# A graph network on one core: sums over edge slots moved from a VectorE reduce to TensorE, with constant waits in the gather loops

## The chip, the cores and the metric

One NeuronCore of one Trainium2 chip runs the whole program in one launch. The metric is the device time of that launch in microseconds, the lower the better. The engines have short names in what follows: PE is TensorE, DVE is VectorE, ACT is ScalarE, POOL is GpSimd, SP is SyncE. Each has its own instruction queue; they wait for each other by semaphores only.

## The reference, cut to what matters

A graph of 6250 nodes and 206,250 edges (each of 100,000 random pairs in both directions and a loop on every node), sorted by destination, passes through four layers. Layer one is a graph attention layer applied twice (4 heads of 32 columns):

```
h = x @ W;  e = leaky_relu(alpha_s[src] + alpha_d[dst], 0.2)
e_exp = exp(e - segment_max(e, dst)[dst])
alpha = e_exp / (segment_sum(e_exp, dst)[dst] + 1e-16)
out = segment_sum(h[src] * alpha, dst)          # then elu, the second time a residual and a layernorm
```

The second layer sums source rows weighted by edge weights, `segment_sum(x[src] * edge_weight, dst)`, with dense products on both sides of it; the third is an attention layer with 8 heads of 16 columns over the same edges; the fourth is an MLP on each edge, with batch norms over all edges, summed by destination.

## The kernel before, in words

Nodes are ordered by the number of their edges and cut into 49 tiles of 128, one node on a partition. A tile's edges stand in slots, and slots in groups of four (`J`), so that a group is four table rows for each of 128 nodes. A tile has as many groups as its fullest node needs: 15 for the first, then fewer. All tiles together have 428.

`Gather` serves all four gather stages. POOL issues four indirect DMAs a group into a ring of eight groups (L820), waiting for the slots' indices and for `used`, by which the consumer gives a place back. SP waits until a group has landed, raises `landed` (L838) and loads indices for two groups at a time from the DRAM table `slot_src` (L831). That table is laid out by group, then partition, so that an index load reads 16 bytes at a time. The waits compare a semaphore that only grows with a count that is computed in registers (`hold`, L106 and L107, or `wait_ge(sem, g + 1)`).

`attention_pass` is the consumer in layer one and in the attention layer. Its softmax runs: for each group DVE computes scores (L1159 and L1161 in layer one, L1439 and L1441 in the attention layer), weighs the rows of the group before with exponents (`weigh_rows`, L1022, four slots at once), rescales the old sum (`weigh_sum`, L1028) into a fifth slot, takes the maximum (L1037), adds the five slots up (`add_up`, a reduce, L1034), and subtracts the maximum (L1040). ACT takes the exponent (L1094) and copies the new maximum (L1096). At a tile's end DVE divides (L1075 to L1077) and adds the bias (L1165); the next tile begins at L1152. Each tile reads its number of groups and its first group from tables by register loads.

In layer one `DenseRows` works beside it on the second layer's dense weight matrix: for each tile and each chunk of 64 edges a node (here one chunk a tile) it builds one-hot tiles on DVE (L905 to L918), scales them by the edge weights on ACT (L965) and multiplies them on PE (L938) into eight PSUM banks, 32 pairs of slots; each application of layer one does one half of the 64. ACT copies the banks out (L974) and stores them (L978), and fetches the next column of edges (L945). ACT's order in a tile is: the tile's exponents, the store of the tile before, the fetch, the scalings. Nothing else stands between, so the exponents of the next tile come behind the scalings. DVE's order is the tile's groups, then its one-hot tiles. PE has only the dense products.

`edge_stats` is the gather stage of the edge layer: PE transposes gathered rows (L1664), DVE adds (L1645) and takes statistics (L1650), ACT stores. `sum_by_source` multiplies the stored weight matrix with the rows.

## Time and profile before

| | us |
|---|---|
| median of 3 runs (13887.12 to 13893.61) | 13889.23 |
| profiled execution | 13903.95 |
| its span, first to last instruction | 13902.3 |
| DVE busy | 8362.2 (60%) |
| POOL busy | 7297.4 (52%) |
| PE busy | 3796.4 (27%) |
| ACT busy | 2966.8 (21%) |

The rows below come from the one profiled execution. Times are microseconds from the span's start unless marked ns. An engine is busy while an instruction works; register, branch, semaphore and DMA-issuing instructions don't count as busy. A group of instructions is written as line, engine, operation, `out<-in`, count; then busy us and mean ns of one; then the idle time of the engine just before them, and what ended it. `<-issue` is idle time for which no releaser is seen. A timeline row is start, duration, engine, line, operation, and merges what follows without a gap (xcount). A name with a q (ACTq, DVEq) is an engine's sequencer.

### The profile page before, as it was taken

What the parts mean: (1) busy time and instruction counts of PE and PEld (TensorE: products, weight loads), DVE (VectorE), ACT (ScalarE), POOL (GpSimd) and SP (SyncE); (2) the same over time, 40 slices, a digit from 0 to 9 for tenths busy, and PEclk for the clock granted to TensorE, in tenths of its full rate; (3) what the DMA queues carried; (4) which work ended last, traced back from release to release, by engine and by line L of the source; (5) the groups of instructions that cost most, each with busy time, mean ns of one, the idle gap of its engine ahead of it and who ended that gap; (6) DMA issues with size and microseconds to landing.
All of it is one profiled execution on the core that took longest, in us unless ns stands there. A gap on an engine that the chain in (4) does not pass through costs nothing. (4 is left out here: it accounts for less than half of the span.)

```text
span 13902.3 us, 141045 instructions
## 1 busy us (share of the span) xinstructions
PE 3796.4 (27%) x15301; PEld 2288.4 (16%) x15400; DVE 8362.2 (60%) x19005; ACT 2966.8 (21%) x8231; POOL 7297.4 (52%) x7734
## 2 busy tenths in 40 slices
PE   2011122223322222233861000000422222229673
PEld 1001112222211222222431000000221111113221
DVE  7663677777657777774024777777533333346785
ACT  0410233333312333331000000000000000007693
POOL 0103777766467776660004777777137777760132
PEclk9999566666655566666975555555655555559996
DMA  0011334434324444442732444444123333337673
GB/s 2 10 21 30 80 92 96 97 97 98 92 59 93 97 95 100 93 102 94 258 135 55 106 106 105 106 106 107 29 66 106 105 105 106 106 99 244 183 218 89
DMA packets 1268796, 1386.52 MB, mean 100 GB/s; under 512 B 501892, under 2 KB 938986, under 8 KB 1255816
## 3 DMA queue, kind: packets, MB, share of 16 engines
q0 software_dynamic: 276128, 650.85, 19.1%
q1 hardware_dynamic: 500200, 404.68, 10.3%
q10 hardware_dynamic: 492416, 330.48, 8.2%
q14 instruction: 43, 0.35, 0.0%
q8 instruction: 9, 0.15, 0.0%
HBM read 1009.64 MB, written 375.70 MB: 100 GB/s over the span
## 5 line engine op out<-in xcount | busy, mean ns | idle before, releaser
L820 POOL DMA_INDIRECT ring<-gat_table,index x3424 | 3277.9, 957 | 1421.4 <-issue 1004.1
L820 POOL DMA_INDIRECT ring<-kv_table,index x1712 | 1739.9, 1016 | 531.5 <-issue 509.9
L820 POOL DMA_INDIRECT ring<-b_table,index x1712 | 1617.0, 945 | 599.0 <-issue 518.5
L1034 DVE TENSOR_REDUCE acc<-prod 128x132 f32<-128x660 f32 (+1 forms) x1284 | 1709.8, 1332 | 5.1
L1022 DVE TENSOR_TENSOR prod<-ring,p 128x528 f32<-128x528 f32 (+1 forms) x1284 | 921.1, 717 | 623.6 <-ACT e L1096 598.4
L938 PE MATMUL pairs<-hot_lo,hot_hi 128*128 128x128 f32 x6272 | 949.4, 325 | 1238.1 <-ACT hot_lo L965 1237.7
L1094 ACT ACTIVATE p<-x 128x20 f32<-128x20 f32 (+1 forms) x1284 | 286.7, 223 | 4350.1 <-DVE x L1040 4350.1
L965 ACT ACTIVATE hot_lo<-hot_lo,wt 128x128 f32<-128x128 f32 x3136 | 927.9, 387 | 999.5 <-remote 981.7
L938 PEld LDWEIGHTS pairs<-hot_lo,hot_hi 128*128 128x128 f32 x6272 | 924.7, 239 | 1290.5 <-issue 1289.1
L932 PE MATMUL pairs<-nil 128*128 128x512 bf16 x686 | 342.3, 598 | 2315.3 <-ACT dstage L974 2267.2
L1922 PE MATMUL e<-r,fc 128*128 128x512 f32 x1712 | 894.1, 626 | 289.5 <-ACT r L1934 133.5
L1645 DVE TENSOR_TENSOR tb<-bt,att 128x512 f32 x428 | 295.9, 691 | 1111.4 <-PE bt L1664 1054.0
L1664 PE MATMUL bt<-ident,ring 128*128 128x128 f32 x1712 | 465.2, 427 | 1683.5 <-SPq L838 1657.3
L1837 POOL DMA_DIRECT2D running<-run x432 | 232.6, 539 | 997.5 <-DVEq L1887 580.3
L712 PE MATMUL tp<-ident,stage 128*128 128x128 f32 x294 | 73.5, 427 | 2442.0 <-DVEq L699 2390.4
L1934 ACT ACTIVATE r<-tb,coef 128x512 f32<-128x512 f32 x854 | 674.6, 809 | 135.1 <-DMA tb<-kept 103.0
L1664 PEld LDWEIGHTS bt<-ident,ring 128*128 128x128 f32 x1712 | 306.1, 217 | 1842.9 <-issue 1842.9
L577 POOL DMA_INDIRECT layer_out<-by_node,node x49 | 46.3, 944 | 1018.5 <-PEq L86 1003.9
L1254 PE MATMUL fsum<-mat,xs 128*128 128x448 f32 x1372 | 545.1, 549 | 116.4 <-DMA ring<-gat_table,index 89.8
L918 DVE TENSOR_TENSOR hot_lo<-lo,ramp 128x512 f32<-128x512 f32 x784 | 563.1, 718 | 0.0
L1439 DVE TENSOR_TENSOR qk<-ring,qt 128x544 f32<-128x544 f32 x428 | 309.3, 723 | 393.1 <-SPq L838 369.4
L916 DVE TENSOR_TENSOR hot_hi<-hi,ramp 128x512 f32<-128x512 f32 x784 | 533.8, 681 | 3.4
(343 smaller groups left out, 8128.7 us busy)
## 6 DMA issues: line engine op xcount, KB each, us to landing
tb<-kept SPq DMA_DIRECT2D x856, 256.0 KB, 3.0
dense_weights<-dstage ACTq DMA_DIRECT2D x196, 1024.0 KB
mat<-dense_weights SPq DMA_DIRECT2D x98, 1568.0 KB, 6.2
kept<-tb ACTq DMA_DIRECT2D x432, 256.0 KB, 2.2
ring<-gat_table,index POOLq DMA_INDIRECT x3424
running<-run POOLq DMA_DIRECT2D x432, 64.0 KB, 2.9
ring<-kv_table,index POOLq DMA_INDIRECT x1712
ring<-b_table,index POOLq DMA_INDIRECT x1712
```

The costliest lines, as they stand in the source:

```text
L820: pool.indirect_dma_start(self.ring[:, at, :], None, self.table, bass.IndirectOffsetOnAxis(self.index[:, at:at + 1], 0)).then_inc(self.g_s ...
L916: dve.tensor_tensor(self.hot_hi[:, four, :], self.hi[:, four].unsqueeze(2).broadcast_to(shape), ramp, ALU.is_equal)
L918: dve.tensor_tensor(self.hot_lo[:, four, :], self.lo[:, four].unsqueeze(2).broadcast_to(shape), ramp, ALU.is_equal).then_inc(self.marked[b ...
L932: pe.matmul(self.ps[:, b, :], self.nil[:, 0:P], self.nil[:, :], start=True, stop=False, skip_group_check=True)
L938: mm = pe.matmul(self.ps[:, b, i * P:(i + 1) * P], self.hot_hi[:, 4 * b + i, :], self.hot_lo[:, 4 * b + i, :], start=False, stop=False, sk ...
L965: last = act.activation(self.hot_lo[:, i, :], self.hot_lo[:, i, :], ACT.Copy, scale=self.wt[:, i:i + 1])
L1022: dve.tensor_tensor(by_head(prod[:, 0:J, :]), by_head(ga.group(g)[:, :, 0:VB]), p5[:, 0:J, :].unsqueeze(3).broadcast_to([P, J, heads, dim ...
L1034: return dve.tensor_reduce(acc[:, :], prod[:, :, :].rearrange("p s c -> p c s"), AX.X, ALU.add)
L1254: mm = pe.matmul(acc[:, m, 0:MM], xs[:, u, :], mat[:, u, m * MM:(m + 1) * MM], start=start, stop=start, skip_group_check=True)
L1664: mm = pe.transpose(bt[:, r, j * P:(j + 1) * P], ga.ring[:, (first + r) * J + j, :], k.ident[:, :])
L1922: pe.matmul(e1[:, r, :], fc[:, :], r4[:, r, :], start=True, stop=True).then_inc(product, 1)
L1934: act.activation(r4[:, slot, :], tb[:, slot, :], ACT.Relu, bias=coef[:, 1:2], scale=coef[:, 0:1]).then_inc(relued, 1)
```

## The change

Five edits, made together.

1. In `attention_pass` the reduce over five slots goes. `prod` has two buffers, the sum stands in two PSUM banks (`acc`), and PE adds with five products by the identity matrix, four as soon as the rows are weighed and the fifth when the old sum is rescaled. DVE gives the ring's place back after the rescaling, reads the old sum from PSUM, and at a tile's end waits for PE.
2. PSUM has eight banks, so `DenseRows` keeps four: `PAIRS` goes from 32 to 16, and each application of layer one works through two units of 16 pairs a tile instead of one of 32. The column is fetched once for each unit, and the first unit is stored between the two.
3. In the gather loops a wait is for a constant, and takes what it waited for off the semaphore (`claim`). The first group and first chunk of a tile are no longer read from tables but counted in a register (`Running`).
4. `slot_src` is laid out by partition, so that an index load is 64 contiguous bytes a partition and covers four groups, and the writes of the slot stage are 256 contiguous bytes.
5. The same waits are changed in `edge_stats`, `edge_regather`, `build_slots` and `sum_by_source`.

The diff, cut to its core:

```diff
 NBLK = NP // BLK
-PAIRS = 32
+PAIRS = 16
 QUADS = PAIRS // 4
...
+
+def claim(eng, sem, n=1):
+
+    eng.wait_ge(sem, n)
+    eng.sem_inc(sem, -n)
 
...
-        self.index = s.sb("index", [P, RING * J], I32)
+        self.index = s.sb("index", [P, 2, R * J], I32)
...
-        hold = Hold(pool, self.turns)
-
-        def round_(first, turn, group):
-            for r in range(first, first + R):
-                if r % 2 == 0:
-                    hold(self.i_sem[r // 2], 16 * (turn + 1))
-                hold(self.used, group + r - first + 1)
+        def round_(half):
+            claim(pool, self.i_sem[half], 16)
+            for r in range(half * R, half * R + R):
+                claim(pool, self.used)
                 for j in range(J):
-                    at = r * J + j
-                    pool.indirect_dma_start(self.ring[:, at, :], None, self.table,
-                                            bass.IndirectOffsetOnAxis(self.index[:, at:at + 1], 0)
+                    at = (r % R) * J + j
+                    pool.indirect_dma_start(self.ring[:, r * J + j, :], None, self.table,
+                                            bass.IndirectOffsetOnAxis(self.index[:, half, at:at + 1], 0)
                                             ).then_inc(self.g_sem[r], 16)
...
     def load_index(self, sp, half, group):
-        sp.dma_start(self.index[:, half * 2 * J:(half + 1) * 2 * J].rearrange("p (g j) -> p g j", j=J),
-                     self.slots[ds(group, 2), :, :].rearrange("g p j -> p g j")).then_inc(self.i_sem[half], 16)
+        sp.dma_start(self.index[:, half, :], self.slots[:, ds(group * J, R * J)]).then_inc(self.i_sem[half], 16)
 
...
-        def round_(first, turn, group):
-            for r in range(first, first + R):
-                sp.wait_ge(self.g_sem[r], 16 * J * (turn + 1))
+        hold = Hold(sp, self.sp_turns)
+
+        def round_(half, turn, following):
+            for r in range(half * R, half * R + R):
+                hold(self.g_sem[r], 16 * J * (turn + 1))
                 sp.sem_inc(self.landed, 1)
-                if r % 2 == 1:
-                    self.load_index(sp, r // 2, (group + RING + r - first - 1).with_bounds(min_val=0, max_val=GMAX - 2)
-                                    if group is not first else RING + r - 1)
+            self.load_index(sp, half, following)
...
+class Running:
+
+
+    def __init__(self, k, eng, largest):
+        self.eng, self.largest, self.reg = eng, largest, eng.alloc_register(k.name("running"))
+        eng.reg_mov(self.reg, 0)
+
+    def value(self):
+        return self.eng.snap(self.reg, min_val=0, max_val=self.largest)
+
+    def advance(self, n):
+        self.eng.reg_add(self.reg, self.reg, n)
+
...
     def chunks(self, eng, t):
-        n = eng.value_load(self.k.chunks[0:1, ds(t, 1)], min_val=1, max_val=EROWS)
-        c0 = eng.value_load(self.k.chunk0[0:1, ds(t, 1)], min_val=0, max_val=EROWS)
-        return c0, n
+        return eng.value_load(self.k.chunks[0:1, ds(t, 1)], min_val=1, max_val=EROWS)
...
-        part = slice(self.half * PAIRS, (self.half + 1) * PAIRS)
-        c0, n = self.chunks(dve, t)
-        with dve.Fori(c0, c0 + n):
-            take(dve, self.col_in, 16)
-            for b in range(QUADS):
-                take(dve, self.used[b])
...
-            c.reset()
+        shape = [P, 4, P]
+        n = self.chunks(dve, t)
+        for u in self.units:
+            part = slice(u * PAIRS, (u + 1) * PAIRS)
+            with dve.Fori(0, n):
+                take(dve, self.col_in, 16)
+                for b in range(QUADS):
+                    take(dve, self.used[b])
...
+    def pe_tile(self, pe, t):
+        n = self.chunks(pe, t)
+        for u in self.units:
             for b in range(QUADS):
                 take(pe, self.bank_free[b])
                 pe.matmul(self.ps[:, b, :], self.nil[:, 0:P], self.nil[:, :], start=True, stop=False,
                           skip_group_check=True)
-            with pe.Fori(c0, c0 + n):
+            with pe.Fori(0, n):
                 for b in range(QUADS):
                     take(pe, self.built[b])
...
-    def act_chunks(self, act, t):
-
...
+    def act_weigh(self, act, again):
+
+        take(act, self.col_free)
+        self.act_fetch(act, again)
+        for b in range(QUADS):
+            take(act, self.marked[b])
+            for i in range(4 * b, 4 * b + 4):
+                last = act.activation(self.hot_lo[:, i, :], self.hot_lo[:, i, :], ACT.Copy,
+                                      scale=self.wt[:, i:i + 1])
+            last.then_inc(self.built[b], 1)
+
+    def act_tile(self, act, t):
+
+        n = self.chunks(act, t)
+        row = self.row.value()
+        for u in self.units:
+            if u != self.units[0]:
+                self.act_store(act, t, u - 1)
+            with act.Fori(0, n) as i:
+                self.act_weigh(act, ((row + 1 + (i + 1) % n) if u != self.units[-1] else (row + 2 + i))
+                               .with_bounds(min_val=0, max_val=EROWS + T + 1))
+        self.row.advance(n)
+
...
-        prod = s.sb("prod", [P, J + 1, VB])
-        acc = s.sb("acc", [P, VB])
+        prod = s.sb("prod", [P, 2, J + 1, VB])
+        acc = s.ps("acc", [P, 2, 512])
...
+        def total(g):
+            return acc[:, ds(g % 2, 1), 0:VB]
+
+        def weighed(g):
+            return prod[:, ds(g % 2, 1), :, :].rearrange("p q s c -> p (q s) c")
 
...
-                dve.wait_ge(p_ready, g + 1)
-                dve.tensor_tensor(by_head(prod[:, 0:J, :]), by_head(ga.group(g)[:, :, 0:VB]),
+                claim(dve, p_ready)
+                dve.tensor_tensor(by_head(weighed(g)[:, 0:J, :]), by_head(ga.group(g)[:, :, 0:VB]),
                                   p5[:, 0:J, :].unsqueeze(3).broadcast_to([P, J, heads, dim + 1]),
-                                  ALU.mult).then_inc(ga.used, 1)
-
-            def weigh_sum():
-
-                return c.go(dve.tensor_tensor(by_head(prod[:, J:J + 1, :]),
-                                              acc[:, :].rearrange("p (s h c) -> p s h c", s=1, h=heads),
+                                  ALU.mult).then_inc(rows_weighed, 1)
+
+            def weigh_sum(g):
+
+                claim(dve, added)
+                last = c.go(dve.tensor_tensor(by_head(weighed(g)[:, J:J + 1, :]), by_head(total(g + 1)),
                                               p5[:, J:J + 1, :].unsqueeze(3).broadcast_to([P, 1, heads, dim + 1]),
                                               ALU.mult))
-
-            def add_up():
-                return dve.tensor_reduce(acc[:, :], prod[:, :, :].rearrange("p s c -> p c s"), AX.X, ALU.add)
+                return last
...
-                g0, n = bounds(t)
-                start(dve, c, t, acc, e5[:, J, :], work)
-                dve.wait_ge(ga.landed, g0 + 1)
+                n = dve.value_load(k.groups[0:1, ds(t, 1)], min_val=3, max_val=GMAX)
+                g0 = first_group.value()
+                start(dve, c, t, flat2(total(g0 + 1)), e5[:, J, :], work)
+                dve.sem_inc(added, 1)
+                claim(dve, ga.landed)
...
-                    weighed = weigh_sum()
+                    rescaled = weigh_sum(g - 1)
                     c.until(scored)
                     highest = take_maximum()
-                    c.until(weighed)
-                    add_up()
+                    c.until(rescaled)
+                    dve.sem_inc(sum_weighed, 1)
+                    dve.sem_inc(ga.used, 1)
                     c.until(highest)
                     off_maximum()
-                    c.until(highest)
                     c.reset()
-                weigh_rows(g0 + n - 1)
-                c.until(weigh_sum())
-                c(add_up())
-
-                a3 = acc[:, :].rearrange("p (h c) -> p h c", h=heads)
+                last = g0 + n - 1
+                weigh_rows(last)
+                c.until(weigh_sum(last))
+                dve.sem_inc(sum_weighed, 1)
+                dve.sem_inc(ga.used, 1)
+                claim(dve, added)
...
+            def add_group(g):
+                claim(pe, rows_weighed)
+                for j in range(J):
+                    pe.matmul(flat2(total(g)), k.ident[:, :], flat2(weighed(g)[:, j:j + 1, :]), start=(j == 0),
+                              stop=False)
+                claim(pe, sum_weighed)
+                pe.matmul(flat2(total(g)), k.ident[:, :], flat2(weighed(g)[:, J:J + 1, :]), start=False,
+                          stop=True).then_inc(added, 1)
+
+            if rows_of is None:
+                with pe.Fori(0, pe.value_load(k.total[0:1, 0:1], min_val=1, max_val=GMAX)) as g:
+                    add_group(g)
+            else:
+                rows_of.pe_begin(pe)
+                first_group = Running(k, pe, GMAX)
+                with pe.Fori(0, T) as t:
+                    n = pe.value_load(k.groups[0:1, ds(t, 1)], min_val=3, max_val=GMAX)
+                    g0 = first_group.value()
+                    with pe.Fori(g0, g0 + n) as g:
+                        add_group(g)
+                    first_group.advance(n)
+                    rows_of.pe_tile(pe, t)
...
-                rows_of.act_chunks(act, 0)
+                rows_of.act_tile(act, 0)
                 with act.Fori(1, T) as t:
                     exponents(act.value_load(k.groups[0:1, ds(t, 1)], min_val=3, max_val=GMAX))
-                    rows_of.act_store(act, t - 1)
-                    rows_of.act_chunks(act, t)
-                rows_of.act_store(act, T - 1)
+                    rows_of.act_store(act, t - 1, rows_of.units[-1])
+                    rows_of.act_tile(act, t)
+                rows_of.act_store(act, T - 1, rows_of.units[-1])
...
-                       lambda s2: DenseRows(k, s2, turned, dense, 0 if elu else 1), spill)
+                       lambda s2: DenseRows(k, s2, turned, dense, (0, 1) if elu else (2, 3)), spill)
...
-                    hold(ga.used, g + 1 + RING)
-                    hold(free, g + 1)
+                    claim(dve, turned)
+                    dve.sem_inc(ga.used, 1)
+                    claim(dve, free)
...
-        slot_src = dram("slot_src", (GMAX, P, J), I32)
+        slot_src = dram("slot_src", (P, GMAX * J), I32)
```

## Rows read from the trace of the kernel before

**Rows 1.** Windows view, three gather stages: stretch: length, busy (count) by engine, PEclk, DMA, GB/s.
```profile
1404.00:3800.00 2396.00, 637.00 (x3426) 494.29 (x3476) 1747.20 (x4466) 780.66 (x2790) 1639.78 (x1712) 0.60 0.40 94
...
7554.00:9832.00 2278.00, 0.00 (x0) 0.00 (x0) 1692.86 (x3339) 144.60 (x858) 1739.89 (x1712) 0.50 0.42 105
10307.00:12456.00 2149.00, 465.15 (x1712) 306.11 (x1712) 786.55 (x2245) 0.00 (x0) 1617.02 (x1712) 0.50 0.39 105
```

**Rows 2.** Lines view, POOL's gathers by table.
```profile
L820 POOL DMA_INDIRECT ring<-gat_table,index x3424 | 3277.9, 957 | 1421.4 <-issue 1004.1 <-DVE prod L1022 396.3 <-DMA index<-slot_src 20.9
L820 POOL DMA_INDIRECT ring<-kv_table,index x1712 | 1739.9, 1016 | 531.5 <-issue 509.9 <-DVE prod L1022 11.6 <-DMA index<-slot_src 10.0
L820 POOL DMA_INDIRECT ring<-b_table,index x1712 | 1617.0, 945 | 599.0 <-issue 518.5 <-DMA index<-slot_src 77.8 <-PE bt L1664 2.7
```

**Rows 3.** Timeline, DVE, one group inside a tile of layer one.
```profile
2015.06 0.71 DVE L1022 TENSOR_TENSOR prod<-ring,p 128x528 f32<-128x528 f32 x1 [0.57 <-ACT e L1096]
...
2016.02 0.18 DVE L1037 TENSOR_REDUCE newmax<-e 128x4 f32<-128x20 f32 x1
2016.13 1.32 DVE L1034 TENSOR_REDUCE acc<-prod 128x132 f32<-128x660 f32 x1
2017.37 0.17 DVE L1040 TENSOR_TENSOR x<-e,newmax 128x20 f32<-128x20 f32 x1
...
2018.19 0.73 DVE L1022 TENSOR_TENSOR prod<-ring,p 128x528 f32<-128x528 f32 x1 [0.57 <-ACT e L1096]
```

**Rows 4.** Timeline, DVE, a tile's end to the next one's; then its products counted.
```profile
1978.65 0.72 DVE L1022 TENSOR_TENSOR prod<-ring,p 128x528 f32<-128x528 f32 x1 [0.66 <-ACT e L1096]
...
1981.00 0.17 DVE L1075 TENSOR_SCALAR rden<-acc 128x4 f32<-128x4 f32 x1
...
1981.86 0.29 DVE L1165 TENSOR_TENSOR layer_out<-layer_out,brow 128x128 f32 x1
1984.71 0.18 DVE L905 COPY wt<-col 128x32 f32<-128x32 f32 x1 [2.56 <-remote]
...
1985.92 0.69 DVE L916 TENSOR_TENSOR hot_hi<-hi,ramp 128x512 f32<-128x512 f32 x1
...
1995.23 0.72 DVE L918 TENSOR_TENSOR hot_lo<-lo,ramp 128x512 f32<-128x512 f32 x1
...
2033.92 0.29 DVE L1165 TENSOR_TENSOR layer_out<-layer_out,brow 128x128 f32 x1
...
L1022 DVE TENSOR_TENSOR prod<-ring,p 128x528 f32<-128x528 f32 x10 | 7.2, 718 | 6.7 <-ACT e L1096 6.7
```

**Rows 5.** Timeline, ACT, between the exponents of two tiles.
```profile
1978.23 0.19 ACT L1096 ACTIVATE e<-newmax 128x4 f32<-128x4 f32 x1
...
1982.78 4.39 ACTq L978 DMA_DIRECT2D dense_weights<-dstage  x2
1990.37 2.23 ACTq L945 DMA_DIRECT2D col<-turned  x1
1992.72 9.46 ACT L965 ACTIVATE hot_lo<-hot_lo,wt 128x128 f32<-128x128 f32 x32 [10.24 <-remote]
2002.09 0.20 ACT L1094 ACTIVATE p<-x 128x20 f32<-128x20 f32 x1
```

**Rows 6.** Source view, loop turn on DVE's sequencer; timeline, two semaphores between operations.
```profile
L1054 DVEq FUSED_REGOPS  x2: 51/72/92, 2016.3 to 2016.8; - x2
...
11001.56 0.69 DVE L1650 BATCH_NORM_STATS2 stats<-tb 128x6 f32 x1 [0.24 <-DVE tb L1645]
```

**Rows 7.** Timeline, PE, dense products; windows view, the first 3.9 us.
```profile
1994.15 9.34 PE L938 MATMUL pairs<-hot_lo,hot_hi 128*128 128x128 f32 x64 [10.92 <-ACT hot_lo L965]
...
1994.10:1998.00 3.90, 3.85 (x20) 3.85 (x21) 1.85 (x3) 3.90 (x15) 2.99 (x4) 0.56 0.48 138
```

**Rows 8.** DMA issues: size of one, us to landing.
```profile
dense_weights<-dstage ACTq DMA_DIRECT2D x196, 1024.0 KB
...
slot_src<-outs SPq DMA_DIRECT2D x49, 32.0 KB, 5.6
```

156 lines of the change are left out of this document (69 added, 87 removed).

## The prediction, made before the changed kernel was seen

> **What bounds the kernel now.** I read the busy time by stage first [rows 1]. Four stages gather one table row per edge slot: two of layer one (1404 to 3800 us, and its like from 3946 to 6370), the attention layer's (7554 to 9832) and the edge layer's (10307 to 12456). They are two thirds of the span, and the change lies in them. In each, POOL issues 1712 gathers. In the last two nothing but POOL counts: a gather takes 0.95 to 1.02 us and the next begins 0.30 later [rows 2], and 1712 x 1.25 = 2140 of 2149 us is the whole edge stage. In layer one the same 1712 gathers need (3277.9 + 1421.4 - 396.3) / 2 = 2152 us, but the first of its stages lasts 2396 [rows 1] and the second some 30 more, and POOL stood 396.3 us waiting for DVE's release of the ring [rows 2]. So there the consumer sets the end.
>
> The consumer is a chain through DVE and ACT. Inside a tile one group costs 3.12 us from one `prod` product to the next [rows 3]: product (0.71), the old sum's rescaling, maximum, the five-term reduce (1.32), subtraction, ACT's exponent, next product. From tile end to tile end with ten groups it is 52.06 us [rows 4]; 52.06 - 10 x 3.12 = 20.9 us is the price of a tile outside its groups. The average tile has 1712 / 4 / 49 = 8.73 groups, so the chain wants 20.9 + 27.2 = 48.1 us and POOL 8.73 x 5.0 = 43.9. The two cross at 11 groups.
>
> What fills the 20.9 us is ACT [rows 5]. From its last exponent copy (ends 1978.42) to the next tile's second-stage exponent (2002.09) are 23.67 us: eight copies out of PSUM (4.0), two store issues (4.4), the tile's table loads (3.2), the issue of the column fetch (2.2) and 32 scalings (9.46). DVE has its first one-hot tile under way at 1985.92 [rows 4] and is not late.
>
> **The change part by part.**
>
> *The reduce goes.* L1034 costs 1.32 us of 3.12 [rows 3]. It isn't all gained. Behind the maximum (which ends 1.14 after the product starts) DVE now raises two semaphores; such a pair takes 0.24 with its hand-off [rows 6], so the subtraction can start at 1.3. Then the loop turns: its two register updates ran hidden under the reduce, at 2016.3 and 2016.8 [rows 6]; with the reset ahead of them and the branch between I count 0.75, now laid open. Two claims of 0.1 and the ring's address arithmetic (0.14 to 0.2) follow before the next product: 1.3 + 0.75 + 0.5 = 2.55 us. From below it is bounded by ACT's round trip alone, 0.82 from subtraction to product [rows 3]: 1.3 + 0.82 = 2.1. From above by 3.12, or more if TensorE is late. I take 2.65, near the first count, for a little waiting on TensorE. The gain is 0.47 us for each group but the first of a tile: 428 - 49 = 379 of them a stage, 178 us.
>
> *TensorE adds.* Five identity products of 132 columns a group, each two MATMULs. An fp32 MATMUL of 128 columns follows its predecessor by 9.34 / 64 = 0.15 us on average [rows 7], over a stretch whose first 3.9 us had a granted clock of 0.56 [rows 7]: it ran at both levels. Estimated from that, ten cost 1.2 us at the higher clock and 2.2 at the lower. Within a tile that is beside DVE's 2.55, and DVE needs the result only at its next rescaling, some 2.6 after the product ended. At a tile's end nothing covers it: today 2.35 us pass from the last product (1978.65) to the division's start (1981.00) [rows 4]; new it is 0.66 product, 0.35 hand-off, 1.2 to 2.2 and 0.5 to the landing and back, 2.7 to 3.7. I take +1.0 us.
>
> *One table load and several takes fewer.* DVE's 2.56 us between tile end and column copy [rows 4] hold two loads and nine takes; one load (0.7) and four takes (0.4) go. With the +1.0 the first one-hot tile starts where it does today, 7.5 us after ACT's last copy.
>
> *Two units of 16 pairs instead of one of 32.* This is where I expect the loss. The 16 one-hot tiles, 32 scalings and 64 MATMULs stay, but in two halves with a store between, all in ACT's order. Counted from ACT's last exponent copy: first half's marks 7.5 to 12.6 (eight quads took 1985.92 to 1995.95 [rows 4], 1.25 each); ACT's last four scalings end at 13.9; TensorE's last eight MATMULs (0.9 to 1.8 at the two clocks) and its drain make the banks full at 15.8; four copies out take 2.05 and the way to the first issue 0.35: 18.3. Then two store issues and the next fetch. Today the fetch is let go 9.8 us after the first store issue began (1982.78 to 1992.60 [rows 5]), with two stores of 1024 KB before it [rows 8]. With half the bytes I take 5.5; it is at least 4.1 (everything halves and the table loads between are gone) and at most 9.8. So 23.8, and sixteen scalings (9.46 / 2) and a start: 28.7. Against 23.67 that is +5.0 us a tile, 245 a stage. DVE's second half starts when TensorE has released the one-hot tiles at 15.5 and ends at 22.3; today its next tile needs less than the 6.1 us from there to ACT's exponent (1995.95 to 2002.09), and one table load goes; at the most that is 27.7, so ACT stays last.
>
> The Trainium skill, "Perfetto Trace Analysis", section on a DMA instruction through the hardware generator, has the issue slice last until all descriptors are generated. The rows don't quite fit it: of two equal store issues the first took 0.65 and the second the rest of 4.39 [rows 5], so a transfer waits for the one before it. By the page an issue would scale with its descriptors, the 5.5 would be 4.1, and each tile 1.4 us shorter: 137 us less in all. That is the second case below.
>
> *Sum for layer one.* 245 - 178 = +67 a stage; the first tile waits for gathers anyway, so its 14 periods save nothing (+7), and the last tile stores once more after everything (+4): +78, for two stages +156. POOL's need (2152) is below both.
>
> *Attention stage.* DVE is busy 1692.86 / 428 = 4.0 us of each group's 5.3 [rows 1] and POOL waited 11.6 us for it in 1712 gathers [rows 2]; the removed reduce buys nothing, TensorE is idle there. A gather's mean is 1016 ns against 945 in the edge stage [rows 2]: gathers that start under a product of two SBUF tensors are longer. Their phase to DVE shifts by the claims' tenths, which I bound by -100 and +100 us and set at 0.
>
> *Edge stage, source sums, slot table.* Same count of instructions with a constant where an addition was. POOL paces the edge stage (2140 of 2149 us), the source sums wait for their matrices' loads; 0. From above each is bounded by a register addition of some 0.05 us a wait, beside other waits. The index now comes once in four groups (20 us of issues ahead), after two before; an index load is a few us, so nothing waits. The table's write, 49 DMAs, costs 49 x 5.6 = 274 us if all of it were waited for [rows 8]; DVE takes that semaphore late in each tile's work, so I set 0. Each gather stage may start 1 us earlier.
>
> The sum is +156 us on the profiled execution's 13903.95, 14060; against the median shown (13889.23, which is 15 lower) it is 14045.
>
> **Rivals.**
> 1. *Cancelled.* The mechanism as above, but the column fetch is let go 4.1 us after the first store issue, not 5.5. Then +3.6 a tile, 176 a stage against 178 + POOL's share: about +20, 13910. For it: the first store issue, with nothing before it, is short. Against: the fetch of one column took 2.23 though it was issued 3.2 us after the stores.
> 2. *POOL becomes the bound (the other side).* If a group falls to 2.35 us (DVE dispatches the loop turn while the two semaphores wait, so only ACT's trip counts) and a tile's surplus is 3 us, the chain at nine groups is 48.9 + 3 - 8 x 0.77 = 45.7 against POOL's 45.1: POOL's pace is nearly reached, -2.3 us a tile on average, -225, 13665. It decides from where the surplus of a tile falls under 7.7 times the saving of a group. For it: 1.32 is much time and my 0.75 for the turn is read at rest; against: nothing in the rows shortens ACT's second store.
> 3. *TensorE sets the group.* If ten MATMULs with their own waits and addresses need 3.3 us a group (only 2.2 is shown, at the lower clock), DVE waits at each rescaling: +5 and +1.4 a tile, +630, 14520. The attention stage still has 5.3 a group and hides it.
>
> **How the numbers follow.** Forecast 0.40, its own range 13960 to 14140 (+-1 us a tile is +-98); rival 1 0.17; rival 2 0.32; rival 3 0.11. The likeliest is 14045. For 8 in 10 I go from 13720, inside rival 2, to 14320, short of rival 3. About 0.2% (28 us) is what a measurement can tell. Slower: 0.38 + 0.11 + a quarter of rival 1, 0.53. Within: 0.10. Faster: rival 2 and the lower part of rival 1, 0.37.
>
> **What would show it.** Group pitch in layer one (product to product): 2.65 right, 2.1 rival 2, over 3.1 rival 3. ACT from last exponent copy to the next tile's second exponent: 28.7 against 23.67; the span from first store issue to the end of the fetch's: 5.5. A ten-group tile: 52.8 us. POOL's wait for DVE in layer one: up from 396 towards 550; if it falls below 200, rival 2 holds. DVE's busy time loses about 1700 us while the layer-one stages get longer. The attention and edge stages keep 2278 and 2149 within 30 us, else the part on gathers' phase is wrong. The prediction fails if second stores cost ACT less than 3 us a tile, or if a group runs under 2.4.

## The result, and the profile after

The changed kernel takes 14,227.4 us (median of 4 runs, 14,222.4 to 14,238.3) against 13,891.4 beside it: ratio 1.0243, 95% interval 1.023 to 1.0256. It is slower by 336 us; 156 were forecast. The sign held. The time lies inside the 8-in-10 range (13,720 to 14,320) but outside the forecast's own range (13,960 to 14,140), and the size is more than double the forecast. The profiled execution's span is 14,224.0 us, 321.7 over that of before.

The windows view of it, for the two stages of layer one, the attention stage and the edge stage (columns as in [rows 1]):

```profile
1370.00:3979.00 2609.00, 1515.52 (x7599) 1335.31 (x7648) 1292.46 (x4260) 794.61 (x2752) 1650.65 (x1712) 0.73 0.39 87
4162.00:6689.00 2527.00, 1454.43 (x7600) 1277.10 (x7649) 1297.96 (x4261) 795.23 (x2753) 1654.27 (x1712) 0.75 0.40 89
7943.00:10141.00 2198.00, 1099.21 (x4250) 977.60 (x4250) 1188.33 (x2895) 142.60 (x852) 1676.05 (x1711) 0.52 0.41 109
10631.00:12768.00 2137.00, 464.24 (x1708) 305.61 (x1708) 785.68 (x2234) 0.00 (x0) 1614.65 (x1712) 0.50 0.36 106
```

DVE lost 450 us of work in each stage of layer one [rows 1], and both stages got longer. POOL's gathers answer to [rows 2]:

```profile
L820 POOL DMA_INDIRECT ring<-gat_table,index x3424 | 3304.9, 965 | 1811.3 <-issue 922.2 <-POOLq L103 866.7 <-DMA index<-slot_src 20.6
L820 POOL DMA_INDIRECT ring<-kv_table,index x1712 | 1677.1, 980 | 531.5 <-issue 393.7 <-POOLq L103 119.1 <-DMA index<-slot_src 10.2
L820 POOL DMA_INDIRECT ring<-b_table,index x1712 | 1615.6, 944 | 599.9 <-issue 394.0 <-POOLq L103 122.5 <-DMA index<-slot_src 78.5
```

Nothing is new in the edge stage. In the attention stage a gather is 36 ns shorter (980 against 1016 in [rows 2]); in layer one POOL idles 390 us more, and 866.7 us of it now end with a claim of the ring (396.3 with VectorE's release before; about 550 were forecast).

The span cut at the first and last starts of tiles and gathers, with two kernels that the experiments come to. R has constant waits and slot table as changed, but VectorE's reduce and 32 pairs, and 128 idle instructions ahead of its loops in each of three stages. The last column is the changed kernel with the same idle instructions, so that R has something to be held against:

| us | before | R | after | after, with R's idle instructions |
|---|---|---|---|---|
| start to layer one's first tile | 1406.6 | 1382.9 | 1369.8 | 1382.8 |
| first to 49th tile start, first stage | 2355 | 2432 | 2609 | 2591 |
| first to 49th tile start, second stage | 2349 | 2381 | 2527 | 2521 |
| first to last gather, attention | 2260 | 2211 | 2197 | 2203 |
| first to last gather, edge | 2137 | 2140 | 2136 | 2136 |
| everything else | 3394 | 3415 | 3385 | 3404 |

So +254 and +177 in layer one, -37 before it, -63 in the attention stage, -10 elsewhere. The idle instructions add 13 us to the first row and 19 to the last, but the two stages of layer one came out 18 and 6 shorter with them; differences of R in single rows are no surer than that.

Inside layer one, means over 46 tiles of a stage (the second to the 47th), worked out from the starts of DVE's products in the traces. A "distance" is the time from the start of one `prod` product to the start of the next. "Groups" runs from a tile's first product to its last (7.72 distances on average), "between" from there to the next tile's first:

| us a tile | groups | between | first distance | second | middle | last |
|---|---|---|---|---|---|---|
| before | 24.07, 24.08 | 23.97, 23.90 | 3.10 | 3.10 | 3.12 | 3.13 |
| R | 25.66, 24.76 | 24.13, 23.96 | 3.31, 3.20 | 3.32, 3.19 | 3.33, 3.20 | 3.30, 3.28 |
| after | 24.40, 23.02 | 28.88, 28.46 | 2.66, 2.55 | 5.36, 4.87 | 2.84, 2.76 | 2.93, 2.53 |

"Between" rose by 4.9 and 4.6, as forecast (+5.0). "Groups" was to fall by 0.47 x 7.72 = 3.6 us to 20.4, and is 24.4 and 23.0. The timeline of DVE at a tile's start shows where that went; it answers to [rows 3]:

```profile
2619.70 0.71 DVE L1051 TENSOR_TENSOR prod<-ring,p 128x528 f32 x1 [0.43 <-DVEq L103]
...
2622.36 0.71 DVE L1051 TENSOR_TENSOR prod<-ring,p 128x528 f32 x1 [0.29 <-issue]
2622.98 0.17 DVE L1219 SCALAR_TENSOR_TENSOR e<-es 128x16 f32<-128x16 f32 x1
2626.25 0.29 DVE L1058 TENSOR_TENSOR prod<-acc,p 128x132 f32 x1 [3.10 <-DVEq L103]
...
2628.20 0.71 DVE L1051 TENSOR_TENSOR prod<-ring,p 128x528 f32 x1 [0.29 <-issue]
...
2630.85 0.71 DVE L1051 TENSOR_TENSOR prod<-ring,p 128x528 f32 x1 [0.29 <-issue]
```

From product to product 2.66, then 5.84, then 2.65. L103 is the wait-and-decrement; before the rescaling of 2626.25 it held DVE for 3.10 us: the first group's sum wasn't there. TensorE in the same microseconds:

```profile
2616.62 4.92 PE L951 MATMUL pairs<-hot_lo,hot_hi 128*128 128x128 f32 x27
2623.44 1.89 PE L1125 MATMUL acc<-prod,ident 128*128 x8 [1.91 <-DVE prod L1051]
2625.12 0.65 PE L1128 MATMUL acc<-prod,ident 128*128 x2
...
2629.36 1.14 PE L1125 MATMUL acc<-prod,ident 128*128 x8 [1.77 <-PEq L103]
```

The first product was written at 2620.41. TensorE was still on the last tile's pair products (L951, to 2621.54). Then its queue held a drain, the loop turn, the load of the tile's group count (0.31 us) with what belongs to it, and the addresses, and only at 2623.44 did the first addition start; from the last pair product's end to there are 1.91 us in the mean of 96 tiles. The eight additions took 1.89 us where the later eight took 1.14, with a granted clock of 0.57 against 1.00. The profile's releaser ("DVE prod") is misleading there: DVE had been done for 3 us.

ACT between two tiles, to be held against [rows 5]:

```profile
2644.87 0.19 ACT L1154 ACTIVATE e<-newmax 128x4 f32<-128x4 f32 x1
...
2654.65 4.97 ACT L977 ACTIVATE hot_lo<-hot_lo,wt 128x128 f32<-128x128 f32 x16 [7.48 <-DVE hot_lo L929]
2662.60 2.06 ACT L998 ACTIVATE dstage<-pairs 128x512 f32<-128x512 f32 x4 [2.98 <-DMA dense_weights<-dstage]
2664.86 1.44 ACTq L1002 DMA_DIRECT2D dense_weights<-dstage  x2
2666.75 1.87 ACTq L958 DMA_DIRECT2D col<-turned  x1
2668.74 4.78 ACT L977 ACTIVATE hot_lo<-hot_lo,wt 128x128 f32<-128x128 f32 x16 [4.08 <-remote]
2673.80 0.22 ACT L1152 ACTIVATE p<-x 128x20 f32<-128x20 f32 x1 [0.27 <-DVE x L1067]
```

From the last exponent copy's end (2645.06) to the next tile's first exponent are 28.74 us; 28.7 were forecast against 23.67 before.

### The profile page after: what moved, and what is told of

It reads as the page before. It is cut to its first block and busy times, and to the rows that moved or that the text cites. A ratio compares the mean times of both kernels' runs of the same rounds, so it can differ in the third digit from the quotient of the medians.

```text
span 14224.0 us, 189193 instructions
## 1 busy us (share of the span) xinstructions
PE 6647.3 (47%) x28141; PEld 4932.2 (35%) x28240; DVE 7015.3 (49%) x18309; ACT 3019.0 (21%) x8231; POOL 7259.6 (51%) x7734
## 5 line engine op out<-in xcount | busy, mean ns | idle before, releaser
L1125 PE MATMUL acc<-prod,ident 128*128 x10272 | 2287.9, 391 | 2089.2 <-PEq L103 1992.3
L1125 PEld LDWEIGHTS acc<-prod,ident 128*128 128x128 f32 x10272 | 1990.5, 283 | 2373.6 <-issue 2372.7
L820 POOL DMA_INDIRECT ring<-kv_table,index x1712 | 1677.1, 980 | 531.5 <-issue 393.7
L951 PE MATMUL pairs<-hot_lo,hot_hi 128*128 128x128 f32 x6272 | 1163.3, 371 | 1097.5 <-ACT hot_lo L977 1097.5
L951 PEld LDWEIGHTS pairs<-hot_lo,hot_hi 128*128 128x128 f32 x6272 | 1126.9, 283 | 1178.0 <-issue 1178.0
L977 ACT ACTIVATE hot_lo<-hot_lo,wt 128x128 f32<-128x128 f32 x3136 | 957.3, 388 | 1148.0 <-DVE hot_lo L929 747.9
L1051 DVE TENSOR_TENSOR prod<-ring,p 128x528 f32 (+1 forms) x1284 | 915.5, 713 | 370.9 <-issue 189.3
L1128 PE MATMUL acc<-prod,ident 128*128 x2568 | 704.1, 369 | 0.0
L1128 PEld LDWEIGHTS acc<-prod,ident 128*128 128x128 f32 x2568 | 589.7, 279 | 0.0
L1972 PEld LDWEIGHTS e<-r,fc 128*128 128x128 f32 x1712 | 270.8, 190 | 911.0 <-issue 901.0
```

Source lines behind the costliest of these rows:

```text
L820: pool.indirect_dma_start(self.ring[:, r * J + j, :], None, self.table, bass.IndirectOffsetOnAxis(self.index[:, half, at:at + 1], 0)).then ...
L951: mm = pe.matmul(self.ps[:, b, i * P:(i + 1) * P], self.hot_hi[:, 4 * b + i, :], self.hot_lo[:, 4 * b + i, :], start=False, stop=False, sk ...
L977: last = act.activation(self.hot_lo[:, i, :], self.hot_lo[:, i, :], ACT.Copy, scale=self.wt[:, i:i + 1])
L1051: dve.tensor_tensor(by_head(weighed(g)[:, 0:J, :]), by_head(ga.group(g)[:, :, 0:VB]), p5[:, 0:J, :].unsqueeze(3).broadcast_to([P, J, heads ...
L1125: pe.matmul(flat2(total(g)), k.ident[:, :], flat2(weighed(g)[:, j:j + 1, :]), start=(j == 0), stop=False)
L1128: pe.matmul(flat2(total(g)), k.ident[:, :], flat2(weighed(g)[:, J:J + 1, :]), start=False, stop=True).then_inc(added, 1)
```

## The experiments

One thing has to be known to read the numbers. Beside the first 16 runs the kernel before took 16,280 to 16,300 us (beside four of them 16,082), and only beside the last two 13,901, as at first. The first kind is called a slow time here. Each ratio is to the kernel before as it ran beside that run. At slow times the traces have stretches in which DVE's, ACT's and SP's queues give out an instruction every 0.7 us, or none for several microseconds. The distances of the first groups of a tile are mostly free of them: 3.10 and 3.10 at both kinds of time for the kernel before, and for the changed kernel's second distance 5.36 and 4.87 at first, 5.15 and 5.38 at a slow time, so that a few tenths there can be chance.

**The constant waits and the table alone** (e1, R without its idle instructions), and the split alone (e2):

```
-            def add_group(g): ... pe.matmul(flat2(total(g)), k.ident, ...)
+            dve.tensor_reduce(acc, prod, AX.X, ALU.add)      # both kernels
-PAIRS = 16
+PAIRS = 32                                                 # e1 only
```

(shortened: in both kernels the whole loop of VectorE is that of before again, with one product buffer and the ring's place given back at the product; the claims stay)

> The changed kernel with the sum given back to VectorE (the five-term reduce into SBUF) in layer one and in the attention layer, and with one unit of 32 pairs again; kept are the constant waits with decrements, the running group count in a register and the slot table stored by partition. Theory A (the lost time lies in the split and in the sum on TensorE): 13,870 us, between 13,840 and 13,900: the stage that builds the slots about 27 us shorter as in the changed kernel, layer one as before (48 us a tile, 3.12 us from product to product), attention stage 2260 us as before, since its 63 us came from the reduce that went. Theory B (the waits and the table brought the attention stage's gain): the attention stage is already at 2197 us here, and the whole is 13,800 us.

> As the run before it (VectorE's reduce, constant waits, slot table by partition), but with two units of 16 pairs a tile as in the changed kernel: the split's price alone. By the prediction's own term, which the changed kernel's trace bears out at +4.9 us from ScalarE's last exponent copy to its first exponent of the next tile, a tile costs 5 us more than in the run before it: 2 x 49 x 5.0 = +490 and +8 at the two ends, about 14,360 us, from 14,320 to 14,400, and the distance from product to product stays 3.12. If the split is cheaper where no TensorE sum stands in the way (3 us a tile), 14,170 us.

Measured: e1 16,167, ratio 0.9929 (0.9912 to 0.9945); e2 16,552, 1.0167 (1.015 to 1.0184). The split costs 385 us at a slow time, 3.9 a tile, between the 5 and the 3 of the two theories. A second run of e2's kernel gave the same:

> VectorE's reduce back in both places, two units of 16 pairs, constant waits, slot table by partition: the same kernel as e2_reduce_16. On a chip that runs the kernel before in 13,890 us: theory of the split (5 us a tile, 98 tiles, +8, less 27 from the slot stage and less a few from one load fewer) 14,360 us, from 14,320 to 14,400, so that the sum on TensorE would have brought 130 us back in the changed kernel. If the split costs under 3 us a tile without the sum on TensorE: 14,170.

16,547, 1.0164 (1.0147 to 1.0181); a third, k1, 16,401 and 1.0202 (1.0185 to 1.0219) beside a kernel before of 16,082, and 412 us (4.2 a tile) over e1's kernel as it ran there (j1 below):

> VectorE's reduce, two units of 16 pairs: the kernel of e2_reduce_16. On a chip like the first, theory of the split at 5 us a tile: 14,360 us; under 3 us a tile: 14,170. On a chip with slow stretches 16,550 as before.

**The yardstick.**

> The changed kernel unaltered, as the yardstick of this call. The chip of the first four runs executed the kernel before in 16,281 us and not 13,890; in its traces many register instructions and branches of VectorE's and SyncE's queues, 0.03 to 0.2 us long elsewhere, take 0.7 us. If that is a property of the chip in use, this run shows whether the changed kernel (more such instructions on VectorE and TensorE) suffers more from it: then its ratio to the kernel before is over 1.06, as the two variants of it showed (1.067 and 1.081). If the chip is like the first one, 1.024.

17,554 us, 1.0779 (1.0761 to 1.0797). So at slow times the sum on TensorE costs 1,000 us over f1, the same kernel with the reduce, and is no gain. One of its groups on DVE:

```profile
3149.35 0.71 DVE L1051 TENSOR_TENSOR prod<-ring,p 128x528 f32 x1 [2.06 <-issue]
3149.97 0.17 DVE L1219 SCALAR_TENSOR_TENSOR e<-es 128x16 f32<-128x16 f32 x1
3158.27 0.29 DVE L1058 TENSOR_TENSOR prod<-acc,p 128x132 f32 x1 [8.13 <-DVEq L103]
```

The sum it waits for had been complete since 3147.7; the queue itself gave nothing out from 3150.6 to 3157.8.

**What stands ahead of the additions.** TensorE's load of the next tile's group count ahead of the pair products (e3); three of four pair products left out (e4, f2); twelve products of zeros ahead of each unit, to raise the clock (g1); rows and identity in bf16 (g2); e3 and g1 together (g3); all of e3, g1 and g2 (j2).

```
 e3   n = pe.value_load(k.groups[0:1, ds(t, 1)]); g0 = first_group.value()
+     rows_of.pe_tile(pe, t - 1)
      with pe.Fori(g0, g0 + n) as g: add_group(g)
 g1 +  for _ in range(12): pe.matmul(self.spare, self.nil[:, 0:P], self.nil, ...)
 e4 -  for i in range(4):
    +  for i in range(3, 4):
 g2 +  prod = s.sb("prod", [P, 2, J + 1, VB], BF16); ident16 for k.ident
```

> The changed kernel, but TensorE loads the group count of the next tile before the pair products of this one, not behind them, so that the load (1.2 us on TensorE's sequencer between the second unit's end and the first addition) no longer stands ahead of the new tile's additions. Theory Q (the additions stand in TensorE's queue behind the second unit's products, its drain and the load; VectorE waits for them at its second rescaling in a tile): the second distance from product to product falls from 5.4 and 4.9 us (the two stages' means) by about 1.2, 98 tiles make -118 us: 14,110. Theory C (TensorE's own length at the granted clock sets it, the queue does not): the load was beside other work, within 20 us of 14,224.

> The changed kernel with three of every four pair products on TensorE left out (the dense weights are then wrong, and so is what follows from them); one-hot tiles, scalings, copies, stores and additions stay. Theory Q (additions queue behind the pair products): the second distance from product to product in a tile falls from 5.4 and 4.9 us to 3 or less, and ScalarE finds the banks full about 1.7 us after its last scaling of the first unit and not 2.9: 3 us a tile from the one and 1.5 from the other, 98 tiles, about -440 us, 13,790. Theory C (the ten additions of a group are too long at TensorE's granted clock, with or without the products before them): the second distance stays over 4.5 us and only the 1.5 us a tile go, about 14,080 us.

> The changed kernel with three of every four pair products left out on TensorE (dense weights and what follows from them are then other values): the same kernel as e4_few_products. Theory Q (the additions queue behind the pair products): the second distance from product to product of a tile falls from 5.4 and 4.9 us to 3 or less, ScalarE's chain gets 1.5 us a tile shorter, 13,790 us. Theory C (ten additions are too long by themselves at the granted clock): second distance over 4.5, 14,080 us.

> The changed kernel with twelve bf16 products of zeros into a spare PSUM bank ahead of each unit's pair products, where TensorE now waits with nothing to do for 5 to 7 us. Theory K (the pair products are slow because TensorE's granted clock is at 1.2 GHz when they start, 0.213 us from one to the next, and that is what pushes the additions behind): the clock is at 2.4 GHz when the unit starts, its 32 MATMULs take 3.6 us and not 5.9 to 6.8, they keep up with ScalarE's scalings, the banks are full 1.2 us after the last scaling and not 2.9, and the second distance in a tile falls by 2 to 3 us: 3.5 to 4.5 us a tile, -350 to -440 us against the changed kernel (13,830 on a chip like the first). Rival (the clock isn't the cause, or the zeros don't raise it): no tile gets shorter, and the twelve products may delay the unit: same as the changed kernel or up to 100 us more.

> The changed kernel with the weighed rows written as bf16 and added by a bf16 identity: five MATMULs a group and not ten (the sums lose precision). Theory A (the additions' own length decides in the middle and at the end of a tile, the queue behind the pair products only at its start): mean distance in the middle of a tile from 2.84 and 2.76 to 2.6 us, from the last product to the division's start from 3.05 to 2.4, the second distance still over 4: about -2.2 us a tile, -210 us against the changed kernel (14,010 on a chip like the first). Theory B (all of the loss is the additions' length): the second distance falls under 3 as well, -400 us.

> The changed kernel with both: the next tile's group count loaded ahead of the pair products, and twelve products of zeros ahead of each unit. If queue and clock are the two parts of one delay, the second distance from product to product is down to 2.7 us and a tile 4.5 us shorter than in the changed kernel: -440 us, 13,790 on a chip like the first, 100 under the kernel before. If only one of the two acts, the same as that one alone.

> The changed kernel with all three: next tile's group count loaded ahead of the pair products, twelve bf16 products of zeros before each unit, and rows and identity in bf16 (the sums lose precision). If queue, clock and length add up, the second distance from product to product is VectorE's own 2.65 us and the mean in a tile too; on a chip like the first 14,224 - 98 x 3.9 = 13,840 us or less; on a chip with slow stretches about 17,100, like g2_bf16_sum. If something else holds the second rescaling, it stays over 3 us.

| run | us | ratio to before | second distance, two stages | pair products' end behind the last scaling |
|---|---|---|---|---|
| f0, as changed | 17,554 | 1.0779 | 5.15, 5.38 | 2.6 |
| g1, zeros ahead | 17,538 | 1.0752 | 4.76, 4.93 | 2.1 |
| f2, a quarter of the products | 17,376 | 1.0670 | 4.29, 4.36 | 0.9 |
| g2, bf16 sum | 17,160 | 1.0530 | 4.29, 4.39 | |
| e3, early load | 17,597 | 1.0807 | 3.68, 3.64 | |
| g3, e3 and g1 | 17,509 | 1.0743 | 3.18, 3.18 | 2.1 |
| j2, all three | 16,918 | 1.0519 | 2.79, 2.76 | 1.6 |

(e4, the same kernel as f2, 17,399 and 1.0677, distances 4.29 and 4.37.) The times moved by stretches in the later groups, so they show none of the forecasts in microseconds; the second distance is what tells. Each of three things shortens it when it alone is changed: the load moved ahead by 1.5 and 1.7 us, a quarter of the products ahead by 0.9 and 1.0, additions half as many by 0.9 and 1.0. They don't simply add up: 3.3 to 3.7 together, while the second distance lies only 2.5 and 2.8 over the first (2.66 and 2.55 in f0), and after load and zeros the short additions bring 0.4 (g3 to j2) and no longer 0.9. As I read it, they stand in one queue, and what one of them gives back is partly covered by DVE's own work; no run tests that. With all three changes the second distance is 2.79 and 2.76, 0.1 to 0.2 over the first: no other cause is left of any size. Theory C, that the additions' length alone does it, falls: e3 left the additions as they were. Theory Q has the right cause, but in e4 and f2 the distance fell to 4.3 and not to 3. Theory K's forecast (2 to 3 us) failed: the zeros bring 0.4 us. That is not what the clock is worth, for they raise it only in part: of the steps from one pair product to the next some 3,800 are at the 0.21 us of the 1.2 GHz level in f0 and still 2,860 in g1. The products also run behind ACT's scalings (16 in 4.8 us) and can't get far ahead of them. Theory A of g2 was right in that the distance stayed over 4 (4.3), but the additions' length counts at a tile's start too (0.9 us). In j2:

```profile
3117.64 5.46 PE L955 MATMUL pairs<-hot_lo,hot_hi 128*128 128x128 f32 x32 [2.30 <-ACT hot_lo L981]
3123.92 0.62 PE L1132 MATMUL acc<-prod,ident 128*128 x4 [0.82 <-PEq L103]
```

and on DVE at that tile's start:

```profile
3121.84 0.71 DVE L1058 TENSOR_TENSOR prod<-ring,p 128x528 f32 x1 [0.43 <-DVEq L103]
...
3124.51 0.71 DVE L1058 TENSOR_TENSOR prod<-ring,p 128x528 f32 x1 [0.29 <-issue]
...
3125.29 0.30 DVE L1065 TENSOR_TENSOR prod<-acc,p 128x132 f32 x1
...
3127.23 0.71 DVE L1058 TENSOR_TENSOR prod<-ring,p 128x528 f32 x1 [0.29 <-issue]
```

The pair products end at 3123.10 and the additions start 0.8 later, against 1.9 in the changed kernel (e3: 0.77 in the mean); no wait is left ahead of the rescaling.

**TensorE's sum in the attention layer alone** (layer one as in e1), twice:

> Layer one with VectorE's reduce and one unit of 32 pairs a tile, the attention layer with the sum on TensorE as in the changed kernel; constant waits and the slot table by partition in both. If each part acts where the traces say: slot stage -27 us, attention stage -63, layer one as before or up to 0.5 us a tile better (one load and four takes fewer on VectorE, which ends after ScalarE's work in no tile): 13,800 us, from 13,750 to 13,830, under both kernels. If the waits by decrement made layer one slower, over 13,890.

> VectorE's reduce and 32 pairs in layer one, the sum on TensorE in the attention layer: the kernel of f3_mixed. On a chip like the first: 13,800 us if the attention stage's 63 us come from the sum on TensorE, 13,865 if they do not. On a chip with slow stretches 16,470 as before.

16,467, 1.0107 (1.0091 to 1.0124), and 16,298, 1.0136 (1.012 to 1.0153). At slow times it costs 1.8% over e1's kernel, where both layers have the reduce; at a time like the first it wasn't run.

**The kernel before at a slow time** (g0), for its trace:

> The kernel before, for its trace on the chip in use. If the chip is one of those of the first eight runs (16,281 us), its trace shows stretches of some 10 to 25 us in which VectorE's and SyncE's queues take 0.7 us for each instruction, and the 2,390 us over 13,890 lie in them: in layer one mostly, 60 to 66 us a tile against 48, and about 330 us each in the attention and the edge stage. If it is a chip like the first one, 13,890 us and no such stretch.

16,303 us, layer one 66 us a tile. Attention and edge stage are 243 and 462 us longer than at first (330 each were expected). But for one instruction the slow stretches come only once the gathers run. The two views below show the same lines of the edge stage, first g0's, then those of before:

```profile
12441.96 0.69 DVE L1645 TENSOR_TENSOR tb<-bt,att 128x512 f32 x1 [5.45 <-issue]
12444.78 0.69 DVE L1650 BATCH_NORM_STATS2 stats<-tb 128x6 f32 x1 [2.13 <-issue]
```
```profile
10507.47 0.69 DVE L1645 TENSOR_TENSOR tb<-bt,att 128x512 f32 x1 [0.75 <-DVE goes_on L1638]
10508.40 0.69 DVE L1650 BATCH_NORM_STATS2 stats<-tb 128x6 f32 x1 [0.24 <-DVE tb L1645]
```

**More register moves** (j1).

> The kernel of e1_reduce_32 (VectorE's reduce, one unit of 32 pairs, constant waits) with eight register moves more in VectorE's queue in each turn of the group loop, of layer one and of the attention layer, 6,800 in all in layer one and 3,400 in the attention layer; nothing else changes. Theory S (on chips with slow stretches an instruction of VectorE's queue costs 0.7 us in a third of the time and 0.05 otherwise, and VectorE's queue is what the time follows): 8 x 0.7 us in one group of four, some 1.4 us a group over 1,284 groups, +1,000 to +1,800 us against e1_reduce_32 (16,167). Theory N (the slow stretches are an effect and not a cause: the queue waits for something else that lasts the same): under +300 us. On a chip without such stretches eight moves are 0.3 to 0.4 us a group, partly beside ScalarE's exponent: +100 to +250 us in layer one, nothing in the attention layer.

The moves are not in its trace (1,994 MOVEs in VectorE's queue with and without them). At 15,989 us, 0.9951 (0.9934 to 0.9968), it is e1 once more and says nothing of the stretches.

**Loops moved in the program** (l1 is R; l2 the changed kernel), by 128 increments of an unused semaphore.

> The kernel of e1_reduce_32 (0.993 of the kernel before) with 128 increments of an unused semaphore ahead of VectorE's loops in each stage of layer one and of the attention layer: 13 us of work a stage, 39 in all, beside the wait for the first gathers in part. Theory P (the place of the loops in the program sets the slow stretches): its ratio to the kernel before leaves 0.993 by more than 0.01 in either direction. Theory M (the stretches come from other traffic, whatever the place): 0.993 to 0.997.

> The changed kernel with the same 128 increments in each of the three stages. Theory P: its ratio to the kernel before leaves the 1.078 of f0_after by more than 0.01, and if the loops come to lie well it nears the first chip's 1.024. Theory M: 1.077 to 1.082.

Beside these two the kernel before took 13,901 us again, without slow stretches, on the chip that by its number in the record was also f0's: so the stretches don't belong to the chip. By the letter both ratios left theirs as theory P wants, but the kernel before had changed its time too, so the place of the loops stays untested. They answer another question. l2: 14,244 us, 1.0251 (1.0234 to 1.0268): the padding costs 0.08%, some 11 us, less than the interval. l1: 13,949 us beside 13,901, 1.0035 (1.0021 to 1.0049); without padding it would be about 1.0027, an estimate from l2. So the constant waits and the table, which I had at nothing and which at slow times gave 0.7% back (e1), cost some 37 us here. That is the sum of larger terms: -37 before layer one (-24 in the first table, and 13 of padding), +108 in it, -49 in the attention stage; what they leave open, some 10 us, is less than the idle instructions move in single rows. The last was theory B of e1, and it holds for 49 of the 63 us, though its total (13,800) doesn't; theory A's failed in layer one, which isn't as before. In the attention stage the gathers' mean length tells it: 1016 ns before, 987 in R, 980 after, and 29 ns on 1712 gathers are 50 us (341, 298 and 242 of them took over 1 us). The group in R, DVE and then ACT:

```profile
2001.87 0.71 DVE L1215 TENSOR_TENSOR prod<-ring,p 128x528 f32<-128x528 f32 x1 [0.78 <-DVEq L103]
...
2002.90 1.32 DVE L1227 TENSOR_REDUCE acc<-prod 128x132 f32<-128x660 f32 x1
...
2005.17 0.71 DVE L1215 TENSOR_TENSOR prod<-ring,p 128x528 f32<-128x528 f32 x1 [0.73 <-DVEq L103]
```
```profile
2001.25 0.19 ACT L1291 ACTIVATE e<-newmax 128x4 f32<-128x4 f32 x1
```

ACT's copy ends at 2001.44, the product starts at 2001.87, 0.43 later. Before, ACT's copy

```profile
2017.78 0.19 ACT L1096 ACTIVATE e<-newmax 128x4 f32<-128x4 f32 x1
```

ended at 2017.97 and the product started at 2018.19 [rows 3], 0.22 later. The source view says why: before, the wait sat on the address arithmetic of the product itself; with a decrement the wait is an instruction of its own, and the arithmetic comes after it, on the path. Before, then R:

```profile
L1022 DVEq FUSED_REGOPS  x1: 140/140/140, 2018.0 to 2018.0; - x1
L103 DVEq EVENT_SEMAPHORE  x2: 21/21/21, 2001.5 to 2003.6; - x2
L1215 DVEq FUSED_REGOPS  x2: 140/140/140, 2001.6 to 2004.9; - x2
```

Over all groups of a stage the median from copy to product is 0.22 us before and 0.43 and 0.32 in R's two stages: +0.21 and +0.10, just what R's distances are longer. (Why the second stage pays less is open.) In the changed kernel the product starts 0.69 after ACT's copy (2676.53 to 2677.22), but there the wait isn't what holds it:

```profile
L103 DVEq EVENT_SEMAPHORE  x2: 21/21/21, 2676.5 to 2676.8; - x2
L1051 DVEq FUSED_REGOPS  x2: 108/124/140, 2676.9 to 2677.1; - x2
```

DVE's queue comes to this wait only at 2676.80, 0.27 after the copy, since the loop turn and the scores' own wait stand ahead of it. From the wait to the product are 0.42 us, with two address computations, against 0.39 in R's first stage with one.

## Why the prediction was half right

The step that failed is "Within a tile that is beside DVE's 2.55": TensorE's additions are not beside it at the start of a tile. The runs show DVE waiting there for additions that stand in TensorE's queue behind the last tile's products, a drain, the loop turn and a load, and the second distance alone costs some 227 of the 300 us by which the groups of layer one miss the forecast. The sign was right, but by the prediction's own chances slower stood at 0.53, hardly more than even.

*Tile surplus, +5.0 us.* Right in size: "between" +4.9 and +4.6 with TensorE's tile end included. That it came out so well is in part luck. In the tile shown the banks are read 17.5 us after the last exponent copy where I had 15.8, since the scalings end at 14.6 and not 13.9 and the pair products end another 2.7 behind them; the store is issued at 19.8 and not 18.3; from there to the fetch's end are 3.8 us (2664.86 to 2668.62) and not 5.5. The two errors cancel: the fetch is let go at 23.6, forecast 23.8.

*Tile end on TensorE, +1.0.* From last product to division 2.35 before, 3.05 and 3.13 after (medians 2.8): +0.7 and +0.8.

*Group pitch 2.65.* Right for DVE's own chain: the median in the middle of tiles is 2.65 and 2.52. Wrong as a mean. I took TensorE's additions by their length and left out what stands ahead of them in an engine that works in order: the second unit's pair products, the drain, the loop turn, the load. Against 2.65 x 7.72, the groups of a tile take 4.0 us more in the first stage: 2.7 in the second distance, 0.9 in the middle (TensorE catching up, ten MATMULs at 0.22 us each at the 1.2 GHz level, as I read it), 0.3 in the last; in the second stage 2.6, of which 2.2 and 0.6, with 0.2 back. That is 182 and 118 us over the 46 tiles. "Between" gives 24 of them back, and the first and last tiles came out as forecast; the two stages together are 275 us over the forecast. A tile of ten groups takes 57.1 and 54.7 us, forecast 52.8.

*The constant waits at 0.* In layer one they were inside my 2.65 for the changed kernel (claims and arithmetic were counted at 0.5), but R shows what they cost where the old wait was: 0.2 and 0.1 us a group. Against R the sum on TensorE gained 0.66 us a group in the middle's median, not 0.47; the waits had taken the rest before. *Slot table and its stage at 0:* -37; the table's writes land in 1.5 us where it was 5.6 [rows 8], but no run parts the table from that stage's waits. *Attention at 0, bounds -100 to +100:* -63, of which 49 come with the waits and the table (R has the reduce) and some 8 to 14 with the sum (the 8 is against R with the same idle instructions). It is inside the bounds, but over the 30 us that were to tell whether the part on the gathers' phase is right; that part had no sign and no size. *Edge stage at 0:* -1. Right. *DVE's busy time, -1700:* 8362 to 7015, -1347; the reduce had overlapped its neighbours in part.

*Rivals.* Rival 1 (fetch let go at 4.1 us) was right in its step, 3.8, yet the time wasn't saved: the banks came 1.7 us late. Rival 2 fell: POOL waited longer, not less, and the pitch's median stayed at 2.5 to 2.65, not 2.35. Rival 3 had the right engine and the wrong form: no group needs 3.3 us on TensorE, the delay stands at the start of each tile.

*The rule weighed.* From the first store's issue to the fetch's end took 3.8 us with half the bytes, 9.8 before. The Trainium skill, "Perfetto Trace Analysis", section on a DMA instruction through the hardware generator, has the issue slice last until all descriptors are generated. The case that I worked out by it was 4.1, an estimate, and the measured sum is near it. The parts don't follow it: the first store issue took 0.65 us with 1024 KB and 0.63 with 512, so it doesn't go with the bytes; the second took 3.57 and now 0.63. Two table loads (1.25 and 0.90 us) that stood between in the 9.8 are gone as well. And the fetch behind the two stores took 1.87, where the same fetch with no store just before it took 0.35 (2652.54 in the trace). What makes an issue wait for those before it isn't shown.

The sum of what the runs show, on the span: forecast +156, groups of layer one +300, "between" -24, start -37, attention -63, rest -10: +322.

## What to carry to other kernels

Work moved to an idle engine is priced by when that engine gets to it: list what its queue holds at the moment the result is first needed, the loads and drains too, before its own length. A wait that an address computation carries is free of one step; a wait with a decrement is an instruction of its own, and what it used to carry then runs behind it, 0.1 to 0.2 us a group on this chain. And where a change takes more hand-offs between engines, time it more than once: the same two kernels stood 2.4% apart at one time and 7.8% at another.

## What the runs showed of the hardware that was not expected

At slow times every kernel took 16 to 23% longer, with the mean granted TensorE clock little changed (0.632 for the kernel before against 0.655). From the first gather on, DVE, ACT and SP get an instruction every 0.70 us in stretches of 10 to 30 us (3,667 register, branch and semaphore instructions over 0.3 us in g0, 3 in the trace of before), TensorE and POOL hardly ever. What causes it is open: when the place of the loops in the program was moved, there were no stretches with or without it. Kernels with TensorE in the loop of each group lose most (17,554 against 16,547 with the reduce).

Gathers that start while the product L1215 runs are often longer in R: 342 of 395 in layer one took over 1 us (mean 1.18), none of the 880 that began under the reduce (mean 0.946). Before, it was 97 of 378 (mean 1.02) under L1022. It doesn't hold for every product of two SBUF tensors: none of the 603 gathers that began under L929 in R took over 1 us. These counts are worked out from the starts in the traces.
